# One graph layer on one core: routing batches of 7, 6, 6, 4 and 2 tiles in place of 6, 6, 5, 5 and 3, and pad rows split two to six between SyncE and ScalarE

## The reference, cut to what matters

```
tokens = layernorm(x)                       # 3125 x 256
probs  = softmax(tokens @ router_w.T)       # 8 experts
rw, re = top_k(probs, 2); rw = rw / rw.sum
for e in range(8):
    y   = gelu(tokens @ w1[e] + b1[e]) @ w2[e] + b2[e]
    out = out + combine[:, e] * y           # combine holds rw at the two chosen experts
```

## Time and profile before

| | us |
|---|---|
| median of the three timed runs | 1117.56 |
| lowest, highest of them | 1116.75, 1123.33 |
| the profiled execution's own time | 1118.23 |
| its span, first to last instruction | 1116.5 |

### The profile page before, as it was taken

How to read it: one execution, slowest core, us unless ns; L and a number is a source line. 1 busy time by engine, 2 the same in 40 slices (tenths; PEclk the granted TensorE clock), 3 DMA queues, 4 the chain that set the end, 5 groups by cost and what they waited for, 6 DMA issues and landing times.

```text
span 1116.5 us, 20474 instructions
## 1 busy us (share of the span) xinstructions
PE 923.1 (83%) x6778; PEld 689.5 (62%) x6778; DVE 701.8 (63%) x2083; ACT 396.1 (35%) x1044; POOL 771.3 (69%) x562
## 2 busy tenths in 40 slices
PE   4899788978789999999999999998299763599940
PEld 2444334433468878888788878774188652599940
DVE  4799677867866665666656566635566656355525
ACT  3433233322133434344333434330044331366630
POOL 5688888888888888888888888888312336744430
PEclk8799988988989999999989999998599865799975
DMA  9976545455445565656555555443943323344449
GB/s 328 228 140 117 79 42 96 63 78 80 60 51 89 98 99 90 98 89 99 97 90 90 98 98 71 42 42 25 256 145 95 97 65 117 96 131 130 130 119 269
DMA packets 150815, 120.71 MB, mean 108 GB/s; under 512 B 120209, under 2 KB 140053, under 8 KB 147000
## 3 DMA queue, kind: packets, MB, share of 16 engines
q0 software_dynamic: 63840, 29.60, 25.6%
q1 hardware_dynamic: 81150, 76.94, 24.5%
q10 hardware_dynamic: 5722, 12.86, 3.6%
HBM read 74.71 MB, written 45.71 MB: 108 GB/s over the span
## 4 chain that ended last, share of the span: by engine, by line
POOL 46%; PE 16%; issue 15%; DMA 11%; DVE 7%; another core or an unknown queue 2%; SPq 2%; ACT 1%; ACTq 0%; POOLq 0%; DVEq 0%
POOL edge_sums L686 46%; DMA edge_sums<-sums,addr 6%; PE ps L1314 5%; PE ps L1325 4%; PE ps L1239 2%; DMA r2t<-expert_outputs 2%; DMA edge_sums<-r 1%; PE ps L1299 1%; PE ps L1229 1%; DVE r L1608 1%; DMA same<-edge_sums 1%; SPq L579 1%; PE ps L1036 1%; SPq L502 0%
## 5 line engine op out<-in xcount | busy, mean ns | idle before, releaser
L686 POOL DMA_INDIRECT edge_sums<-sums,addr x408 | 634.1, 1554 | 140.8 <-issue 117.9
L848 ACT ACTIVATE r<-ps 128x500 f32<-128x500 f32 (+1 forms) x225 | 126.1, 586 | 111.8 <-PE ps L1102 67.0
L996 PE MATMUL ps<-edges,same 128*128 128x65 f32 x816 | 114.3, 285 | 20.9 <-DVE same L1369 14.2
L996 PEld LDWEIGHTS ps<-edges,same 128*128 128x128 f32 x816 | 102.0, 197 | 43.0 <-issue 32.5
L745 ACT ACTIVATE sums<-ps 128x260 f32<-128x260 f32 x102 | 39.8, 392 | 233.5 <-PE ps L996 124.7
L1369 DVE SCALAR_TENSOR_TENSOR same<-srow,src_f,below 128x128 f32<-128x128 int32 x408 | 116.1, 346 | 4.9 <-DMA srow<-in_src_row 4.7
L1478 DVE TENSOR_TENSOR r2t<-ps,r 125x2048 f32<-125x2048 f32 x50 | 113.2, 2263 | 0.0
L1036 PE MATMUL ps<-r2t,r 125*64 125x512 f32 x400 | 108.0, 678 | 1.3 <-issue 1.3
L1102 PE MATMUL ps<-ident,r2t 125*128 125x125 f32 x800 | 106.2, 276 | 3.0 <-DVE r2t L1478 2.2
L1130 PE MATMUL ps<-r 128*64 128x125 f32 x1600 | 108.1, 277 | 0.0
L1420 DVE TENSOR_TENSOR r2t<-ps,r 125x3840 f32<-125x3840 f32 x25 | 103.8, 4150 | 0.0
(11 more groups left out here) (251 smaller groups left out, 1477.1 us busy)
## 6 DMA issues: line engine op xcount, KB each, us to landing
srow<-in_src_row SPq DMA_DIRECT2D x25, 1024.0 KB
edges<-in_edge_attr SPq DMA_DIRECT2D x26, 512.0 KB
r<-routed_rows SPq DMA_DIRECT2D x56, 129.0 KB, 2.1
edge_sums<-sums,addr POOLq DMA_INDIRECT x408
hpre_rows<-r ACTq DMA_DIRECT2D x25, 250.0 KB
r<-hpre_rows SPq DMA_DIRECT2D x25, 250.0 KB
edge_sums<-r SPq DMA_DIRECT2D x4, 1040.0 KB, 14.7
r2t<-in_ew SPq DMA_DIRECT2D x4, 1024.0 KB, 9.4
```

The source lines that it names most:

```text
L686: pool.indirect_dma_start(out=tables[k], out_offset=bass.IndirectOffsetOnAxis(ap=addr[:, j:j + 1], axis=0), in_=sums[:, j % OR, :], in_off ...
L848: act.activation(phT[0:rows, j // 2 % 2 * 2 + j % 2, :], bank(1 + j % 2, rows, 0, QC * P), ACT.Copy).then_inc(grp_ready[j % 2], 1)
L996: m = mm(bank(b, 128, c0 + k * F, c0 + (k + 1) * F), lhsT=same[:, j % SR, :], rhs=edges[:, h, j % CH, :], start=True, stop=True)
```

## The change

The batches become 7, 6, 6, 4 and 2 tiles. For the batch that ends at tile 22 the parts `weights`, `ranks` and `exps` would fall before iteration 29, which doesn't exist, so they are capped at iteration 28 (T+3) like `place`. SyncE writes the pad rows of experts 0 and 4, ScalarE those of the other six.

```diff
-    BATCHES = ((0, 6), (6, 12), (12, 17), (17, 22), (22, T))
+    BATCHES = ((0, 7), (7, 13), (13, 19), (19, 23), (23, T))
+    SP_PADS = (0, 4)
...
-            for e in range(0, E, 2):
+            for e in SP_PADS:
...
-            tiles(gnn, 4, [(t1 + 6, lambda b=b: exps(b)) for b, (t0, t1) in enumerate(BATCHES[:-1])])
+            tiles(gnn, 4, [(min(t1 + 6, T + 3), lambda b=b: exps(b)) for b, (t0, t1) in enumerate(BATCHES[:-1])])
...
-            for e in range(1, E, 2):
+            for e in (e for e in range(E) if e not in SP_PADS):
...
-            tiles(gnn, 4, [(t1 + 6, lambda b=b: ranks(b)) for b, (t0, t1) in enumerate(BATCHES[:-1])])
+            tiles(gnn, 4, [(min(t1 + 6, T + 3), lambda b=b: ranks(b)) for b, (t0, t1) in enumerate(BATCHES[:-1])])
...
-                between += [(t1 + 4, lead, b), (t1 + 5, follow, b), (t1 + 6, weights, b), (min(t1 + 7, T + 3), place, b)]
+                between += [(t1 + 4, lead, b), (t1 + 5, follow, b), (min(t1 + 6, T + 3), weights, b), (min(t1 + 7, T + 3), place, b)]
```

## The result

| | before | after |
|---|---|---|
| median, us | 1117.54 | 1128.52 |
| lowest to highest | 1113.79 to 1123.33 | 1121.74 to 1135.38 |
| runs | 13 | 13 |
| the profiled execution, us | 1118.23 | 1128.52 |
| its span | 1116.5 | 1126.8 |

The ratio of the medians is 1.0097, 95% interval 1.0075 to 1.0120. The change makes the kernel 11 us slower; the forecast was 1119.1 with a range up to 1127.

The account below looks back on a forecast made before the run. The start of GpSimd's last unbroken scatter burst and its number of scatters were taken to set the scatters' end. Later scatters added 1.5 us, all else 0: 1119.7 profiled, 1119.1 against the median, range 1111 to 1127.

Parts of the forecast that it names:

- Steps 1, 3 and 4: GpSimd's scatters: first burst 3.27 us later, third at 924.2, then 24 unbroken scatters ending at 955.5, +1.5 us.
- Rival B: GpSimd's bursts: the loop's stands don't grow with the burst, so 2.6 us goes, 1116.5; chance 0.2.
- Step 5: Chain from the fourth batch's `lead` to `pad_row`: `pad_row` at 942.5, 3.4 us later, with GpSimd not starved.
- Step 6: Pad writes and the experts' table, at 951: hidden under the scatters, value 0; upper bound 8 us past the scatters.
- a sign of being wrong: At the end of the scatters: ScalarE's last pad packets coming after the last scatter's would show the forecast wrong.
- Rival A: Late hand-offs put `pad_row` at 957.5, GpSimd runs dry, ScalarE's pads end last: about +25 us, 1142; chance 0.15.
- C: GNN loop: shifted bursts miss the hand-offs and TensorE's lost time comes back, 1107.4; chance 0.05.
- D: Before the row load: pads, not batches, set the end; moving two off SyncE gains up to 2 us, 1116; chance 0.05.

Follow-up runs that it names:

- e10: The new batches alone, pads four on SyncE and four on ScalarE, against the kernel before, late hand-offs: ratio 1.0106.
- e14: The kernel before with only the head changed, batches 7, 6, 6, 3 and 3, pads four to four, late hand-offs: 1.0145, 1132.79 us.
- e12: The changed kernel with the third burst of scatters held until `pad_row` is written, late hand-offs: 1.0138 of the kernel before.
- e13: The kernel before with only the tail changed, batches 6, 6, 5, 6 and 2, pads four to four, late hand-offs: 1.0003, 1117.25 us.
- e6: The kernel before with 17 further VectorE operations delaying `pad_row`, so the table falls on GpSimd's residual, prompt hand-offs: 1.0081, 1102.44 us.
- e7: The kernel of e6 with GpSimd's residual also held until the table is written, prompt hand-offs: 1.0031 of the kernel before, 1095.89 us.
- e5: The change itself, second time, prompt hand-offs: 1.0040, 1096.51 against 1091.92 us for the kernel before.
- e11: The changed kernel with GpSimd's residual held until the table is written, late hand-offs: 1.0088 of the kernel before, 1125.67 us.
- e9: The change itself, third time, late hand-offs: 1.0100, 1126.93 against 1116.34 us for the kernel before.
- e2: The pads alone: batches of before, two pads on SyncE and six on ScalarE, prompt hand-offs: 0.9996 of the kernel before.
- e15: The pads alone, again: batches of before, two pads on SyncE and six on ScalarE, late hand-offs: 0.9993 of the kernel before.
- e1: The new batches alone, pads four to each engine, prompt hand-offs: 1.0019, 1095.93 against 1093.64 us for the kernel before.
- e8: The kernel before with three GpSimd clears ahead of each scatter of the first two batches, spacing them out, prompt hand-offs: 1.0187.

## Why the prediction was wrong

**Steps 1, 3 and 4 (the bursts and the end of the scatters)** hold up. The bursts began at 857.35, 893.53 and 925.76; the scatters ended at 956.33, 0.8 us past the forecast. Part of that is luck: the last burst began 1.6 us late, and its 24 scatters took 30.6 us for the 31.3 of the sum. Rival B (the stands don't grow with the burst) falls. By B the second burst would start 31.2 us after the first, as before; by the forecast 33.8. It was 36.2 in the changed kernel (GpSimd's idle time grew from 15.93 to 18.33 us) and 33.4 in e10, which has the same batches.

**Step 5 (the late chain)** is off by 3.3 us. It had `pad_row` at 942.5, and it came at 945.80. Two and a half of that is the start of the fourth `lead`, 925.93 for 923.4: the third `row_idx` was 1.6 us later than forecast, and the sum forgot that the rest of iteration 26 stands between it and the `lead`. For the same reason "the same instructions stand between them now" was wrong. The rest is the chain itself: from `lead` to `pad_row` it took 19.9 us for 18.1 + 1 = 19.1. The two last hand-offs did fall deep into the burst and cost 5.01 + 4.17 - 0.86 - 0.76 = 7.6 us more. The two ahead of them, 1.60 and 4.36 us before, took 0.28 and 0.87, 4.8 us less, and VectorE's own work was 1.0 shorter. The step itself was fair. The statement that GpSimd isn't starved was right, too: the fourth `row_idx` came at 931.39, before its need.

**Step 6 (the pads and the table are hidden)** is the step that failed. "The table moves to 951: hidden" took the table at its old 8.6 us wherever it stood. It measured 21.9 us and ended at 967.74 instead of 951, 11.4 us past the last scatter. Two terms were missing. One is that VectorE's dependent operations wait about 1.2 us each while scatters run (6.6 us here and 11 in e14; none in e12 and e13, where the table lies early in a burst and takes 9.0 and 8.9 us). The other is that the table now meets GpSimd's residual (7.0 us of the table here; e6 against e7: 6.5 us of the kernel). I had read late news from TensorE out of the earlier trace rows and applied it to hand-offs between engines alone, and had never asked which of the table's operations would meet another engine. The rows held a hint: SyncE needs 14.29 us for four pads there, though they wait for no other engine once `pad_row` is written (on a prompt occasion it needs 1.58 us for two, e5). And the trace of before has the price of the residual, which runs there from 954.07 to 967.48: of VectorE's copies for the first steps (L1763) the two beside it, at 962.51 and 964.94, take 2.38 and 2.82 us, the one at 970.78 takes 0.43.

The pads themselves were under-priced as well: six took 15.3 us, not 9.8, and ended 5.9 us after the last scatter, which the prediction had named as a sign of being wrong. With an earlier table they would have released the row load at 963.4 (e11), 7 us past before. The bound of 8 us in step 6 covers that, but the sum took it at 0. In the changed kernel the table is later still, so this costs nothing on top: e10, with four pads each, is as slow as e9.

**Rival A** had the direction and the first half of the cause (the late part of the chain falling deep into an unbroken burst), at 0.15. It is the nearest of the cases, but it didn't come true as written: it priced the pads and not the table, at 25 us, GpSimd never ran dry, and `pad_row` at 945.80 stayed just short of the 946 from which A was to decide. **C** and **D** fall: nothing missed the bursts, and the pads alone change nothing in either kind of occasion (e2, e15).

**The late occasions** were all that the first trace showed. On a prompt one the forecast would have held in kind, with the scatters as what the row load waits for, though not in size: +4.6 us for the change (e5) and +2.3 for the batches alone (e1), against +1.5.

## What to carry to other kernels

When a change makes a stretch of indirect DMAs longer or unbroken, ask what stands beside its far end, and price that work again in its new place; a slack of 8 us is no cover if the work itself can become two to four times as long. Check each small chain that is "hidden" against what GpSimd computes at its new time: in these runs a tensor_tensor, tensor_scalar, cast or copy of VectorE from SBUF beside the residual took up to the length of one of GpSimd's operations (2.9 us), and a reduce its own time. And run a split's halves alone: e13 and e14 told in two runs which half of the batches carried the loss.

## What the runs showed of the hardware

- While scatters run on a late occasion, it isn't only TensorE's news that comes late. VectorE's own dependent operations wait too. In e14, from 14 us into the burst, most of them start 1.40 us apart whatever their length: those of 0.2 us wait 1.0 to 1.3 us, those of 0.62 us 0.8. ScalarE's pads take 2.6 us each (15.31 for six) against 1.0 us (6.01 for six, e5) on a prompt one. In the changed kernel the waits pause between 945.8 and 949.7, 20 to 24 us into the burst, and for about 2 us behind `pad_row` in e9, e10 and e11 too, which I can't explain; so no depth in the burst can be given from which every operation waits.
- The same kernel took 1092 to 1094 us on two occasions and 1116 to 1118 us on the others, and the recorded chip was the same for one of each. The difference arises in this stage: the row load of e5 is at 934.58, that of the changed kernel in the first comparison at 968.49. What makes the hand-offs prompt or late isn't known; it wasn't the edits, as both kernels show both by their times.
- Why scatters in flight delay the other engines at all stays open. e12 shows that they do on a late occasion: with the scatters held back, hand-off and table are as short as on a prompt one. The Trainium skill, "SBUF — State Buffer", section "SBUF: two separate sides", says that DMA and compute can't slow each other; for engines' waits beside these scatters the measurement says otherwise, on late occasions only. What is late there is the start of instructions, and no run shows whether SBUF or its ports have a part in it. Whether scatters spaced further apart would delay them less is untested: the one attempt (e8) fell on a prompt occasion.
